# The gated-delta recurrence of a macaron block: its loop started two chunks later and ended with the output product, register waits replaced by constants, the solver's input loaded in quarters

## The reference, cut to what matters

```python
def _step(Sm, inputs):                       # for each of 8192 tokens, 16 heads of 32
    q_t, k_t, v_t, beta_t = inputs
    Sk = jnp.einsum('bhde,bhe->bhd', Sm, k_t)
    delta = v_t - Sk
    Sm = Sm + beta_t[..., None] * jnp.einsum('bhd,bhe->bhde', delta, k_t)
    o_t = jnp.einsum('bhde,bhe->bhd', Sm, q_t)
    return (Sm, o_t)
...
outputs = jnp.transpose(outputs, (1, 0, 2, 3)).reshape(b, s, D)
return outputs @ wo + bo
```

## Time and profile before

| | |
|---|---|
| median of 3 runs | 3338.19 us (3335.9 to 3341.53) |
| the profiled execution's own time | 3332.84 us |
| its span in the trace | 3331.0 us |
| first stage, to the barrier | about 960 us |
| recurrence (first and last start of a matmul of L1233) | 962.1 to 1741.1 us |
| last stage | from there to the end |
| PE busy over the span | 95% |
| granted TensorE clock, mean | 0.985 of full speed |

### The profile page before, as it was taken

How to read it: one execution, slowest core, us unless ns; L and a number is a source line. 1 busy time by engine, 2 the same in 40 slices (tenths; PEclk the granted TensorE clock), 3 DMA queues, 4 the chain that set the end, 5 groups by cost and what they waited for, 6 DMA issues and landing times.

```text
span 3331.0 us, 149311 instructions
## 1 busy us (share of the span) xinstructions
PE 3179.3 (95%) x68312; PEld 2596.6 (78%) x68312; DVE 1818.1 (55%) x2949; ACT 1405.4 (42%) x3166; POOL 1214.3 (36%) x1227
## 2 busy tenths in 40 slices
PE   6999999999959999999999999999999999999998
PEld 4777777777748888888888778787778887777886
DVE  6787778788649788888522333233333333333323
ACT  5444444454314444444553334333334333333433
POOL 1435564646427677665311222121222202122211
PEclk9999999999979999999999999999999999999999
DMA  3445455454556666666651100101110100111010
GB/s 110 143 147 166 140 170 148 157 153 151 145 186 197 214 210 214 199 195 207 201 182 51 38 22 30 38 26 38 39 38 13 38 34 31 39 38 34 18 38 26
DMA packets 387857, 355.21 MB, mean 107 GB/s; under 512 B 58144, under 2 KB 320672, under 8 KB 384672
## 3 DMA queue, kind: packets, MB, share of 16 engines
q1 hardware_dynamic: 385392, 351.07, 33.9%
q10 hardware_dynamic: 2224, 0.90, 0.2%
HBM read 184.06 MB, written 153.09 MB: 101 GB/s over the span
## 4 chain that ended last, share of the span: by engine, by line
PE 64%; DVE 3%; issue 2%; DMA 1%; ACT 1%; SPq 0%; DVEq 0%; ACTq 0%
PE bank L237 14%; PE bank L235 14%; PE bank L236 14%; PE bank L1233 12%; PE bank L1315 6%; PE bank L1698 2%; PE bank L1689 2%; DMA ringA<-xt 1%; DVE sysf L1478 1%; PE bank L1681 1%; PE bank L1672 1%; DVE tmp L1474 1%; ACT sT L1385 0%; DVE oT_lo L1491 0%; DVE zb L1497 0%
## 5 line engine op out<-in xcount | busy, mean ns | idle before, releaser
L1939 DVE TENSOR_TENSOR glo<-gl,gh 128x512 fp32r<-128x512 f32 x256 | 196.0, 766 | 823.5 <-ACT gh L1817 821.7
L1813 ACT ACTIVATE gl<-bank,b1m 128x512 f32<-128x512 f32 x256 | 176.7, 690 | 736.7 <-PE bank L237 730.9
L235 PE MATMUL bank<-h,w_hi 128*128 128x512 f32 x1024 | 420.6, 411 | 0.1
L235 PE MATMUL bank<-w_hi,gh 128*128 128x512 f32 x1024 | 402.7, 393 | 0.7 <-DVE glo L1939 0.7
L237 PE MATMUL bank<-h,w_lo 128*128 128x512 f32 x1024 | 400.8, 391 | 0.0
L237 PE MATMUL bank<-w_hi,glo 128*128 128x512 f32 x1024 | 400.3, 391 | 0.0
L236 PE MATMUL bank<-h,w_hi 128*128 128x512 f32 x1024 | 398.8, 389 | 0.0
L236 PE MATMUL bank<-w_lo,gh 128*128 128x512 f32 x1024 | 398.4, 389 | 0.0
L1233 PE MATMUL bank<-ringA 32*32 32x32 f32 x16448 | 331.1, 195 | 16.7 <-issue 7.8
L1233 PEld LDWEIGHTS bank<-ringA 32*32 32x32 f32 x16448 | 260.8, 105 | 13.4 <-DMA ringA<-xt 8.5
L1379 ACT ACTIVATE de<-bank 128x64 f32<-128x64 f32 x512 | 114.7, 224 | 322.6 <-PE bank L1233 315.4
(11 more groups left out here) (200 smaller groups left out, 7406.5 us busy)
## 6 DMA issues: line engine op xcount, KB each, us to landing
ringB<-heads_scratch SPq DMA_DIRECT2D x256, 192.0 KB, 3.0
ringA<-heads_scratch SPq DMA_DIRECT2D x257, 128.0 KB
X<-in_L_attn_x SPq DMA_DIRECT2D x16, 1024.0 KB, 10.0
x_scratch<-X SPq DMA_DIRECT2D x16, 1024.0 KB, 4.4
heads_scratch<-vb SPq DMA_DIRECT2D x16, 1024.0 KB, 5.2
heads_scratch<-qk SPq DMA_DIRECT2D x16, 1024.0 KB, 6.8
heads_scratch<-kb SPq DMA_DIRECT2D x16, 1024.0 KB, 5.2
heads_scratch<-kbuf SPq DMA_DIRECT2D x16, 1024.0 KB, 7.3
```

What stands on the lines that cost most here:

```text
L235: e.matmul(o, lhs[0], rhs[0], start=first, stop=False)
L1813: e.activation(gl[k][:, :], bank[1 - k][:, :], ACT.Gelu_apprx_tanh, bias=b1m[:, m:m + 1]).then_inc(a_gl, 1)
L1939: e.tensor_tensor(gh[k][1][:, :], gl[k][:, :], gh[k][0][:, :], ALU.subtract).then_inc(v_gl, 1)
```

## The change

It rewrites the order of PE's loop and the waits around it:

- Chunks 0 and 1 of block 0 are issued ahead of the loop. The loop then has 63 rounds, each with chunks 2 and 3 of a block, chunks 0 and 1 of the next, and the output product as its last work. Chunks 2 and 3 of the last block follow the loop. The product with zeros is gone, as are the keys and values of a 257th chunk.
- `v_olo` becomes two semaphores, counted up by one by DVE and down again by PE in the loop; all waits compare with constants. The wait for `v_z` is gone.
- No matmul waits and updates a semaphore both: the updates move to later matmuls.
- The wait for the next chunk's ringB stands inside the chunk before it.
- `load_system` is cut into four DMAs of 512 KB, at chunks 8, 12, 16 and 20 of 32 in place of 12.

```diff
-            def load_system(s):
+            def load_system(s, quarter):
+                r = slice(quarter * NC // 4, (quarter + 1) * NC // 4)
                 if s >= 2:
                     e.wait_ge(v_turn, 4 * (s - 1))
-                e.dma_start(lt[:, :, :, :], lt_d[s]).then_inc(d_lt, 16)
+                e.dma_start(lt[:, r, :, :], lt_d[s][:, r, :, :]).then_inc(d_lt, 16)
...
-                if c % NC == 12 and c // NC + 2 < NS:
-                    load_system(c // NC + 2)
+                if 8 <= c % NC < 24 and c // NC + 2 < NS:
+                    load_system(c // NC + 2, c % NC // 4 - 2)
...
-            def chunk(j):
-
-                after, before = (j + 1) % 4, (j + 3) % 4
+            def deltas(j, last=False):
+
                 e.wait_ge(a_state[j], 1)
                 made = delta(j, FRONT)
-                made[0].then_inc(d_A[j], -32)
-                made[1].then_inc(a_delta[before], -2)
-                made[2].then_inc(d_B[before], -16)
-                e.wait_ge(d_A[after], 32)
-                keys(after)
+                made[1].then_inc(d_A[j], -32)
+                if not last:
+                    e.wait_ge(d_A[(j + 1) % 4], 32)
+                    keys((j + 1) % 4)
                 e.wait_ge(a_state[j], 2)
                 delta(j, BACK)
-                e.wait_ge(d_B[j], 16)
-
-            def outs_back(j):
-
-                made = out_delta(j, BACK)
-                made[0].then_inc(a_state[j], -2)
-                made[-1].then_inc(p_o, 1)
-
-            def rest(j):
+                return made
+
+            def emptied(made, j):
+
+                made[2].then_inc(a_delta[j], -2)
+                made[3].then_inc(d_B[j], -16)
+
+            def states(j, last=False):
 
                 after = (j + 1) % 4
                 out_state(j)
                 e.wait_ge(a_delta[j], 1)
                 state(j, FRONT)
-                values(after, FRONT)
+                if not last:
+                    values(after, FRONT)
+                    e.wait_ge(d_B[after], 16)
                 out_delta(j, FRONT)
...
+                made = out_delta(j, BACK)
+                made[1].then_inc(a_state[j], -2)
+                made[-1].then_inc(p_o, 1)
...
-            with e.register("out") as out, e.register("done") as done:
-                e.reg_mov(out, 4)
-                e.reg_mov(done, 8)
-                with nc.Fori(0, NBLK, 1, engines=bass.OrderedEngineSet([mybir.EngineType.PE]),
-                             hint_back_edge=True, head_slot={mybir.EngineType.PE: 0}):
-
-                    chunk(0)
-                    e.wait_ge(v_olo, out)
-                    e.reg_add(out, out, 4)
-                    rest(0)
-                    outs_back(0)
-
-                    chunk(1)
-                    rest(1)
-                    e.wait_ge(v_olo, out)
-                    e.reg_add(out, out, 4)
-                    e.wait_ge(v_z, done)
-                    e.reg_add(done, done, 8)
-                    outs_back(1)
-                    out_product(range(12))
-
-                    for j in (2, 3):
-                        chunk(j)
-                        rest(j)
-                        outs_back(j)
+            deltas(0)
+            e.wait_ge(d_B[0], 16)
+            states(0)
+            emptied(deltas(1), 0)
+            states(1)
+            e.wait_ge(v_olo[1], 1)
+
+            with nc.Fori(0, NBLK - 1, 1, engines=bass.OrderedEngineSet([mybir.EngineType.PE]),
+                         hint_back_edge=True, head_slot={mybir.EngineType.PE: 0}):
+
+                made = deltas(2)
+                emptied(made, 1)
+                made[4].then_inc(v_olo[0], -1)
+                made[5].then_inc(v_olo[1], -1)
+                states(2)
+
+                emptied(deltas(3), 2)
+                states(3)
+
+                emptied(deltas(0), 3)
+                e.wait_ge(v_olo[0], 1)
+                states(0)
+
+                emptied(deltas(1), 0)
+                states(1)
+
+                e.wait_ge(v_olo[1], 1)
+                out_product(range(12))
+
+            emptied(deltas(2), 1)
+            states(2)
+            emptied(deltas(3, last=True), 2)
+            states(3, last=True)
...
                 e.wait_ge(p_o, 2 * q + 2)
-                e.wait_ge(p_wo, q // 2 + 1)
+                if q >= 2:
+                    e.wait_ge(p_wo, q // 2)
...
-            e.memset(oh[0][:, :, :].bitcast(F32), 0.0)
-            e.memset(oh[1][:, :, :].bitcast(F32), 0.0).then_inc(v_olo, 8)
+            e.memset(oh[0][:, :, 0:1].bitcast(F32), 0.0).then_inc(v_olo[0], 1)
+            e.memset(oh[1][:, :, 0:1].bitcast(F32), 0.0).then_inc(v_olo[1], 1)
```

More of the change, by code:

```diff
@@ L1107, in macaron @@
         a_delta, a_state = sems("a_delta0 a_delta1 a_delta2 a_delta3"), sems("a_state0 a_state1 a_state2 a_state3")
-        v_turn, v_sol, v_back, v_olo, v_z = sems("v_turn v_sol v_back v_olo v_z")
+        v_turn, v_sol, v_back, v_z = sems("v_turn v_sol v_back v_z")
+        v_olo = sems("v_olo0 v_olo1")
         o_s0, o_sol, o_yb = sems("o_s0 o_sol o_yb")
@@ L1120, in sp_delta @@
         def sp_delta(e):
-            def load_system(s):
+            def load_system(s, quarter):
+                r = slice(quarter * NC // 4, (quarter + 1) * NC // 4)
                 if s >= 2:
                     e.wait_ge(v_turn, 4 * (s - 1))
-                e.dma_start(lt[:, :, :, :], lt_d[s]).then_inc(d_lt, 16)
+                e.dma_start(lt[:, r, :, :], lt_d[s][:, r, :, :]).then_inc(d_lt, 16)
             def load_a(c):
-                chunk = c if c < CHUNKS else c - 4
-                s = chunk // NC
+                s = c // NC
                 if c >= 4:
@@ L1134, in load_a @@
                     e.wait_ge(v_back, 4 * s)
-                e.dma_start(ringA[:, c % 4, RK:RV + 1, :], heads_d[chunk, :, K2:V2 + 1, :]).then_inc(d_A[c % 4], 16)
+                e.dma_start(ringA[:, c % 4, RK:RV + 1, :], heads_d[c, :, K2:V2 + 1, :]).then_inc(d_A[c % 4], 16)
                 if s:
                     e.dma_start(ringA[:, c % 4, RX, :],
-                                xt[s % 2][:, chunk % NC, :, :].rearrange("p n i -> p (n i)")).then_inc(d_A[c % 4], 16)
+                                xt[s % 2][:, c % NC, :, :].rearrange("p n i -> p (n i)")).then_inc(d_A[c % 4], 16)
                 else:
                     e.dma_start(ringA[:, c % 4, RX, :],
-                                xt_d[chunk].rearrange("p n i -> p (n i)")).then_inc(d_A[c % 4], 16)
+                                xt_d[c].rearrange("p n i -> p (n i)")).then_inc(d_A[c % 4], 16)
             def load_b(c):
@@ L1145, in load_b @@
                     e.wait_ge(p_o, c - 3)
-                elif c == 3:
-                    e.wait_ge(p_delta, 1)
                 e.dma_start(ringB[:, c % 4, :, :], heads_d[c, :, Q2:B2 + 1, :]).then_inc(d_B[c % 4], 16)
@@ L1163, in sp_delta @@
                 load_a(c)
-                if c < 3:
-                    load_b(c)
+                load_b(c)
             for k in range(NF):
                 e.dma_start(stage2[k], a["L0_attn_wo"][k * P:(k + 1) * P, :]).then_inc(d_stage[k], 16)
-            load_system(1)
+            for quarter in range(4):
+                load_system(1, quarter)
             e.dma_start(bo[:, :], row(a["L0_attn_bo"], D)).then_inc(d_bo, 16)
             e.dma_start(ln2[:, :], a["L0_attn_ln2_scale"].rearrange("(g p) -> p g", p=P), **SHORT).then_inc(d_bo, 16)
-            load_b(3)
             load_x1(0)
@@ L1176, in sp_delta @@
                 c = 4 * blk
-                if c + 4 <= CHUNKS:
+                if c + 4 < CHUNKS:
                     load_a(c + 4)
-                if c + 4 < CHUNKS:
                     load_b(c + 4)
@@ L1308, in rest @@
                 state(j, BACK)
-                values(after, BACK)
+                if not last:
+                    values(after, BACK)
+                made = out_delta(j, BACK)
+                made[1].then_inc(a_state[j], -2)
+                made[-1].then_inc(p_o, 1)
             def out_product(ks):
@@ L1362, in pe_delta @@
                 m.then_inc(p_ht3, 1)
-            e.wait_ge(v_olo, 2 * CHUNKS + 8)
-            e.wait_ge(v_z, 2 * CHUNKS + 8)
+            e.wait_ge(v_olo[0], 2)
+            e.wait_ge(v_olo[1], 2)
             out_product(range(12))
@@ L1449, in turn @@
                 if n == 0:
-                    e.wait_ge(d_lt, 16 * (s + 1))
+                    e.wait_ge(d_lt, 64 * (s + 1))
                 if s:
@@ L1490, in low @@
                 e.wait_ge(a_ohi, q + 1)
-                e.tensor_tensor(pair_half(oh[1], q), pair_bank(q), pair_half(oh[0], q), ALU.subtract).then_inc(v_olo, 4)
+                e.tensor_tensor(pair_half(oh[1], q), pair_bank(q), pair_half(oh[0], q), ALU.subtract).then_inc(v_olo[q % 2], 1)
             def add_out(blk):
                 i = blk % 2
-                e.wait_ge(p_wo, blk + 2)
+                e.wait_ge(p_wo, blk + 1)
                 e.wait_ge(o_yb, blk + 1)
@@ L1563, in pool_delta @@
```

(2 more changed lines are left out.)

2 lines of the change are left out of this document (removed).

## The result

| | before | after |
|---|---|---|
| median of 4 runs each | 3339.79 us (3335.9 to 3341.53) | 3308.26 us (3307.38 to 3309.91) |
| the profiled execution's own time | 3332.84 us | 3309.91 us |
| its span in the trace | 3331.0 us | 3308.1 us |
| start of round 6 (its chunk 0) | 1061.37 us | 1065.91 us |
| rounds 6 to 51 | 542.1 us | 515.5 us |

The changed kernel takes 0.9908 of the time before, 95% interval 0.9891 to 0.9925: 31.5 us less, where 37 were forecast; 3308 lies in the range. Totals are therefore taken from the medians, and places from the traces.

The account below looks back on a forecast made before the run. PE was taken to bound most of the recurrence, DVE rounds 2 to 5. Rounds -41, loads -9, DVE's lateness +6 and first-time code +7 gave -37 us: 3338.2 to 3301 us, forecast range 3288 to 3312, with rivals 3286 to 3319.

Parts of the forecast that it names:

- What bounds the kernel: In the recurrence PE sets the pace over most of it; DVE paces rounds 2 to 5 and is close behind after.
- The back edge: At chunk 3's end the branch and PE's idle time vanish under the product: 0.37 us a round, lower bound 0.2.
- it doesn't do what it says: Rival: the back edge's pause is ACT's late state and returns elsewhere; about -15 us, time 3323; chance 0.04.
- Registers and separate waits: In chunks 0 and 1, register additions save 0.10 and 0.14 us a round; two separate wait instructions save 0.10.
- My lower bound for a round: Least saving per PE round, given as 0.4 us, or 23 us over the 58 rounds from 6 to 63.
- The loads: Quartered system loads end 6.5 us of PE's ringA waits, plus 2.5 for the clock: 9 us, bounds 4 and 14.
- DVE gets less room: In the 47 dense rounds DVE's `low` is late oftener for PE: 6 us lost, bounds 0 and 23.
- First-time code: Chunks ahead of and behind the loop run once, with fetch waits: 1.5 plus 5.5, together 7 us lost, bounds 0 and 18.
- DVE's bound zone follows and absorbs it: Argument that DVE pacing rounds 2 to 5 softens fetch waits ahead of the loop; used against a 3314 us rival, chance 0.07.
- The rule of the Trainium skill: Rival: PE's fetches at 16 KB boundaries are mostly hidden, so first-time code costs 0; time 3294; chance 0.15.
- ringB: Its earlier wait costs nothing: 4.8 us from issue against 3.0 to landing; rival that it is late, 3375 us, chance 0.03.

Follow-up runs that it names:

- e4: The changed kernel with DVE solving one of its three groups, two of the four groups left unsolved: 3282.75 us.
- e10: The changed kernel with its loop turned back (64 rounds, product of zeros) and DVE solving one of its three groups: 3290.76 us.
- e2: The changed kernel with its loop turned back: 64 rounds from chunk 0, product of zeros, chunk 3 at the loop's end; the rest kept: 3309.13 us.
- e1: The kernel before with only load_system cut into quarters at chunks 8, 12, 16 and 20: 3325.75 us.
- e3: The changed kernel with semaphore updates back on the waiting matmuls, so four separate wait instructions a round: 3306.46 us.
- e8: The changed kernel with the solver's input in one 2 MB load at chunk 12 again: 3320.22 us.
- e9: The changed kernel with the first system loaded ahead of chunks 2 and 3 and wo, its solving put forward, and the product behind chunk 2's deltas: 3281.82 us.
- e6: The changed kernel with the product one delta later, between the deltas of chunk 2 and its outputs: 3288.91 us.

## Why the prediction was right, and where its steps were off

*What bounds the kernel.* Right: PE over most of it, DVE in rounds 2 to 5 and close behind from 6 on. What I did not ask is how much room DVE has at the one place where PE waits for it.

*The back edge, 0.37 us a round.* The mechanism held: the branch vanished under the product, the waits of 18.3 us put down to ACT's state at the chunks' starts went, and the rival that "it doesn't do what it says" fell. The size was right for a PE without other waits, 0.34 over the 46 rounds in e4 against e10. In a quiet round it was 0.21 on average (10.98 to 10.77), because chunks 0 and 1 are shorter there behind the pause; I had compared one chunk with its neighbour, not the whole round. With DVE's full work only 0.12 was left in the 46 rounds. This is the term that failed: 58 x 0.37 = 21 us forecast; between e2 and the changed kernel the 46 rounds give 5.4 and the eleven behind them 2.3.

*Registers and separate waits, 0.34 us together.* e1 to e2 shows 0.36 in quiet rounds, 0.29 in the 46, and 16.6 us of the medians against 19.7. The share of 0.10 for separate waits was wrong: e3 puts it at nothing. The registers and the other waits had all of it: 0.16 in chunk 1, within its end of 0.24, and 0.14 in chunk 0, just over its end of 0.13. My lower bound for a round was added up wrongly: 0.2 for the edge and nothing for the rest make 0.2, or 12 us in 58 rounds, not 0.4 and 23.

*The loads, 9 us.* 12.7 alone and 12.0 back in the changed kernel. I counted the waits of one trace, 6.5 us without the one that stays. Its own time, 3332.84 us, lay below all timed runs, and e8's trace shows 13.3 us in six waits, of which one, of some 2 us, stays. The 3.7 us more than booked were luck for the total: with 9 us the time would have been near 3312, the upper end of my forecast.

*DVE gets less room, 6 us.* Too small. The wait for `oT_lo` rose by 12 us (4.9 to 16.8) where the forecast had it rise to 11. 2 of the 12 are there in e1 (7.0) and e2 (6.6), and 10 came with the turn. Nor did I expect DVE to get slower: its 420 solver steps took 364.1 us before, 374.2 in the changed kernel and 383.5 in e9 (197.2 + 186.3).

*First-time code, 7 us.* In all about right, its place wrong. Ahead of the loop I booked 1.5 us; round 6 starts 4.5 later than before, and 6.5 and 6.2 later in the two comparisons with an unturned loop. I had argued that DVE's bound zone follows and absorbs it. It does not: rounds 2 to 5 took 51.0 us before and 49.9 after, since DVE's stream is itself tied to the chunks' outputs and idles for them (15.0 us of `oT_lo` waiting for `oT_hi` in the rows above, 9.5 before), so a late PE makes DVE start late. Behind the loop I booked 5.5; from the start of round 63 to the last stage's first matmul it is 19.1 us against 15.8, 3.2 more, with one wait of 2.10 us. Ten fetches ahead and 14 in all were foreseen (some 13), and nothing was fetched in between. The rule of the Trainium skill that the prediction named ("Runtime: NRT & Kernel Launch", "Instruction fetch mechanics"), by which such fetches are mostly hidden, does not hold here: the waits beside the ten fetches add up to 21.9 us.

*ringB.* No wait on it, with landings at 3.2 us against 4.8 to spare:

```profile
ringB<-heads_scratch SPq DMA_DIRECT2D x188, 192.0 KB, 3.2
```

*The sum by the experiments.* By medians against the same runs of the kernel before, the loads give 12.7 us, the registers and waits 16.6 and the turn 0.9 (e2 to the changed kernel), 30.2 in all; the 31.5 of the result are against other runs of it. The forecast was 37. Inside the turn the traces show 15.5 + 2.8 us gained in rounds 6 to 62 by e10 and e4, 10 to 11 of which DVE's lateness takes back, 6.5 lost ahead of round 6 and 3.4 behind the loop. That makes a loss of some 2 us where the medians have a gain of 0.9, and neither is clear of the noise. The turn as such gave nothing in this kernel: its 18 us are matched by some 20 us of DVE's lateness and one-time code.

## What to carry to other kernels

When a pause is taken out of the engine that sets the pace, price it over the whole round and ask which deadline of the next engine comes earlier by it; moving the product by 0.7 us was worth 19 us here (e6), 11.6 of them named waits for that deadline, as much as the pause itself where nobody is late (18 us). An engine with a tenth of its time free can still be late at one place. Work peeled off a loop of short instructions is code that runs once, and ahead of its loop this kernel pays for each 16 KB of it with a wait of about 2 us (21.9 us for ten).

## What the runs showed of the hardware

- In quiet rounds chunk 0 takes 1.80 us behind the back edge's pause and 1.89 without it, for the same matmuls (e2 and the changed kernel). Over rounds 6 to 51 there is no such gain, 1.93 against 1.90. Why is not settled.
- A block's worth of new code cost 1.84 to 2.11 us of waiting where plain code follows on (991 to 1007 us) and 5.89 us at the loop's first instruction, while the body, once fetched, ran 63 rounds without a fetch.
- POOL's 420 solver steps took 331.3 us beside DVE's full work and 217.2 us in e4, where DVE's steps work on a third of the data and POOL's code is the same. So POOL's steps are slowed by what DVE does at the same time.
- The same 420 solver steps on DVE took 5% longer when the rounds were 8% shorter (364.1 to 383.5 us). POOL is busy for 391.70 of 526 us in e6, and ACT's and the DMAs' share rose as well; which of them slows DVE was not tried, though e4 points to POOL without proving it.
